# Attention beside an octonion feed-forward: 123 entries of the maxima ahead of attention, not 52, a new order in attention, and a fourth set of queries, keys and values

## The reference

```python
xn = _layernorm(x, axis=-1)
# attention
qkv = einsum('bsd,od->bso', xn, w_qkv) + b_qkv      # 32 heads of 16
scores = einsum('bqhd,bkhd->bhqk', q, k) / sqrt(16) + alibi
attn = softmax(where(causal, scores, -1e9))
s = einsum('bsd,od->bso', attn @ v, w_out) + b_out
# feed-forward, weights ternary, octonion structure
h = silu(gate) * up
g = silu(oct_ternary_linear(h, w_down))
return x + s * g
```

## Time and profile before

| what | value |
|---|---|
| median of 3 runs | 898.8 us (896.7 to 901.62) |
| the profiled execution | 896.58 us, span 894.8 us |
| PE busy | 816.8 us, 91% of the span |
| DVE busy | 630.1 us, 70% |
| ACT busy | 479.1 us, 54% |
| POOL busy | 112.7 us, 13% |
| granted clock of TensorE, mean | 0.979 |
| row maxima on DVE, lines 1083 and 1087 | 512 and 256 instructions, 221.9 and 158.6 us |
| exponentials on ACT, line 806 | 320 instructions, 311.8 us |

### The profile page before, as it was taken

How to read it: one execution, slowest core, us unless ns; L and a number is a source line. 1 busy time by engine, 2 the same in 40 slices (tenths; PEclk the granted TensorE clock), 3 DMA queues, 4 the chain that set the end, 5 groups by cost and what they waited for, 6 DMA issues and landing times.

```text
span 894.8 us, 16075 instructions
## 1 busy us (share of the span) xinstructions
PE 816.8 (91%) x5938; PEld 355.9 (40%) x5938; DVE 630.1 (70%) x1795; ACT 479.1 (54%) x631; POOL 112.7 (13%) x124
## 2 busy tenths in 40 slices
PE   5899989999999999999899899999999999998866
PEld 4445444444444334334343333333333333333322
DVE  5475786643242463463799999999999999992498
ACT  4453265333232221231587778887877778789310
POOL 3123131323031121121000000000000000000042
PEclk8899999999999999999799999999999999999989
DMA  7735322243102000000022111222222111264658
GB/s 218 210 107 177 129 72 82 100 123 94 48 1 71 24 1 24 24 0 30 19 63 75 56 55 55 70 75 75 66 71 75 50 58 56 72 193 125 226 192 314
DMA packets 68199, 80.01 MB, mean 89 GB/s; under 512 B 26630, under 2 KB 38918, under 8 KB 67608
## 3 DMA queue, kind: packets, MB, share of 16 engines
q1 hardware_dynamic: 67992, 78.71, 27.8%
q0 software_dynamic: 128, 0.27, 0.2%
HBM read 46.95 MB, written 31.73 MB: 88 GB/s over the span
## 4 chain that ended last, share of the span: by engine, by line
PE 64%; DVE 16%; issue 8%; DMA 7%; SPq 4%; ACT 2%; POOL 0%; ACTq 0%; DVEq 0%
PE psum L1389 13%; PE psum L1349 9%; PE psum L1412 9%; PE psum L1413 8%; DVE mshown L1083 5%; PE psum L1423 4%; PE psum L1424 4%; DVE mx L1087 4%; PE psum L1365 3%; DMA o_scr<-osum 2%; PE psum L1249 2%; PE psum L1251 2%; PE psum L1250 2%; DMA r_scr<-den 2%; PE psum L1261 2%
## 5 line engine op out<-in xcount | busy, mean ns | idle before, releaser
L806 ACT ACTIVATE probs<-psum,exp_scale 128x1024 f32<-128x1024 f32 (+1 forms) x320 | 311.8, 1028 | 78.4 <-PE psum L1374 48.5
L1083 DVE CUSTOM_DVE_ANT_0 mshown<-psum,ahead 128x384 bf16<-128x384 f32 (+3 forms) x512 | 221.9, 487 | 15.2 <-PE psum L1349 13.9
L1349 PE MATMUL psum<-QKs 51*128 51x512 f16 (+3 forms) x768 | 194.1, 333 | 16.0 <-DVE mx L1083 6.2
L1389 PE MATMUL psum<-probs,Vs 128*32 128x512 f32 (+3 forms) x1536 | 162.3, 510 | 19.8 <-ACT osum L812 17.6
L1087 DVE TENSOR_REDUCE mx<-psum 128x1 f32<-128x512 f32 x256 | 158.6, 683 | 3.2 <-PE psum L1349 2.2
L1365 PE MATMUL psum<-QKs 53*128 53x512 f16 (+3 forms) x768 | 139.5, 331 | 3.3 <-ACT probs L806 3.1
L1412 PE MATMUL psum<-X,room 128*128 128x512 f16 (+1 forms) x352 | 133.9, 380 | 0.0
L1413 PE MATMUL psum<-X,room 128*128 128x512 f16 (+1 forms) x352 | 133.4, 379 | 0.0
L1349 PEld LDWEIGHTS psum<-QKs 51*128 51x128 f16 x768 | 53.2, 94 | 166.4 <-DVE mx L1083 87.8
L831 ACT ACTIVATE room<-psum,gate_half 128x512 f32<-128x512 f32 (+1 forms) x44 | 30.2, 687 | 110.0 <-PE psum L1413 109.9
L1117 DVE SCALAR_TENSOR_TENSOR room<-room,psum 128x512 f32<-128x512 f32 (+1 forms) x44 | 30.2, 687 | 71.3 <-ACT room L831 71.3
(11 more groups left out here) (148 smaller groups left out, 934.4 us busy)
## 6 DMA issues: line engine op xcount, KB each, us to landing
o_scr<-osum SPq DMA_DIRECT2D x32, 256.0 KB, 2.9
QKs<-q_scr SPq DMA_DIRECT2D x96, 64.0 KB
QKs<-k_scr SPq DMA_DIRECT2D x96, 64.0 KB
q_scr<-qk_stage SPq DMA_DIRECT2D x16, 256.0 KB, 2.2
k_scr<-qk_stage SPq DMA_DIRECT2D x16, 256.0 KB, 2.2
v_scr<-v_stage SPq DMA_DIRECT2D x16, 256.0 KB, 2.0
Vs<-v_scr SPq DMA_DIRECT2D x16, 256.0 KB
g_scr<-room SPq DMA_DIRECT2D x16, 256.0 KB, 2.0
```

What stands on the lines that cost most here:

```text
L806: nc.scalar.activation(probs[n % PSLOTS][:, 2 * pair:2 * pair + 2, 0:COLS[n]], s_bank[pair][:, :, 0:COLS[n]], ACT.Exp, scale=exp_scale[:, ...
L1083: last = nc.vector.tensor_tensor_reduce(out=mshown[at % 2][:, cols], in0=m_bank[bank][:, cols], in1=ahead[:, CH - keys:], scale=1.0, scala ...
L1349: last = nc.tensor.matmul(tile[:, hh, :], Qs[s][rows, pair + hh, qb * P:(qb + 1) * P], Ks[s][rows, pair + hh, k0:k0 + keys], start=(hh == ...
L1389: last = nc.tensor.matmul(pv_bank[32 * h:32 * h + 32, CH - cols:CH], Vs[s][:, kb, h::QH], probs[n % PSLOTS][:, h, at:at + cols], start=(kb ...
```

## The change

`SLOTS` is 4. The fourth slot of queries and keys is a view of `X16[0]`; its constants and `load(3)` are issued in the last chunk of the gated stage, once the third chunk's gate and up tiles are done. Group t (from 1 to 12) issues `load(t + 3)`.

`early` now runs up to number 39 of group 2's entries, without entry 5 of group 0. It is given out in runs of three after every second tile, and the last run stands after the last tile. Group t has 37 entries "maximum" in place of 42: group 0 begins at entry 39 of group 2, group 1 at entry 34 of group 3, and each starts five earlier than the one before it, down to entry 11 of group 15 in group 14, which has 32 entries as before. `GROUP` has 67 letters in place of 72, and P, S and M stand in a new order. The work itself, every piece, read, exponential and product, is unchanged.

```diff
--- before.py
+++ after.py
@@ -28,7 +28,7 @@
 HALF = P // 2
 PAIRS = QH // 2
 M_SCALE = 2.0 ** 15
-SLOTS = 3
+SLOTS = 4
 INV_SCALE = 4.0
 
 X_SCALE = 2.0 ** 8
@@ -126,7 +126,6 @@
 FTILES = 2 * HT + TT
 FSIG = HT + TT
 FRING = 5
-F_FIRST = 2 * FTILES
 
 
 def position(u, i):
@@ -139,14 +138,23 @@
     return u * NITEM - 1 + i, (i - 1) % MRING
 
 
-GROUP = "MPMMPSMMSMPMMSSMMMSSMMPMSMMSPMMSMPMM" \
-        "SMSMMPMSMMMMSSMPMMSPMMSSMMPMMSMSMMSM"
+GROUP = "MPMSMMPMSMSMPMMSSMMPMSMMSPMMSMPMM" \
+        "SSMMPMSMMSMPSMMSMPMSMMSMPMSMSMMSMS"
+AHEAD = [LEAD + (QUADS - 2 - t) * (NITEM - GROUP.count("M")) for t in range(QUADS - 1)]
+
+
+def line(t):
+
+    start = (t + 1) * NITEM + AHEAD[t] if t < QUADS - 1 else QUADS * NITEM
+    return start
 
 
 def group_order(t):
 
     scores = [(n, pair) for n in range(NST) for pair in range(2)]
-    items = [(t + 1, i) for i in range(LEAD, NITEM)] + [(t + 2, i) for i in range(LEAD)]
+    items = [divmod(i, NITEM) for i in range(line(t), line(t + 1))] if t < QUADS - 1 else []
+    if t == QUADS - 2:
+        items.append((QUADS, ROWS_AT))
     products = [(t - 1, n) for n in range(NST - LAG, NST)] + [(t, n) for n in range(NST - LAG)]
     out = []
     for kind in GROUP:
@@ -154,21 +162,21 @@
             out.append(("scores", t, *scores.pop(0)))
         elif kind == "P":
             out.append(("products", *products.pop(0)))
-        else:
+        elif items:
             out.append(("maximum", *items.pop(0)))
-    return [w for w in out if w[1] >= 0 and (w[0] != "maximum" or w[1] < QUADS or w[1:] == (QUADS, ROWS_AT))]
+    return [w for w in out if w[1] >= 0]
 
 
 def work_order():
 
-    early = [(0, i) for i in range(NITEM) if i != ROWS_AT] + [(1, i) for i in range(LEAD)]
+    early = [divmod(i, NITEM) for i in range(line(0)) if i != ROWS_AT]
     tiles = [(j, p) for j in range(NCH) for p in range(FTILES)]
     order, given = [], 0
     for n, tile in enumerate(tiles):
         order.append(("ffn", *tile))
-        due = max(n + 1 - F_FIRST, 0) * len(early) // (len(tiles) - F_FIRST)
-        order += [("maximum", *x) for x in early[given:due]]
-        given = max(given, due)
+        if tile[1] % 2 and len(tiles) - n <= 2 * -(-len(early) // MRING):
+            order += [("maximum", *x) for x in early[given:given + MRING]]
+            given += MRING
     for t in range(QUADS):
         for w in group_order(t):
             order.append(w)
@@ -221,7 +229,8 @@
 
         OW = alloc(top, "OW", [P, 2, KT, D], f16)
         X16 = [alloc(top, f"X16{i}", [P, 2, KT, CH], f16) for i in range(2)]
-        QKs = [alloc(top, f"QKs{i}", [P, 2, PAIRS, S], f16) for i in range(SLOTS)]
+        QKs = [alloc(top, f"QKs{i}", [P, 2, PAIRS, S], f16) for i in range(SLOTS - 1)]
+        QKs.append(X16[0][:].rearrange("p a k t -> p (a k t)").rearrange("p (a h t) -> p a h t", a=2, h=PAIRS))
         Qs, Ks = ([x[:, i] for x in QKs] for i in range(2))
         Vs = [alloc(top, f"Vs{i}", [P, KB, 2 * QH * HD], f32) for i in range(SLOTS)]
         mx = [alloc(top, f"mx{i}", [P, 2, PAIRS, KB], f32) for i in range(2)]
@@ -530,18 +539,21 @@
             for i in range(2):
                 sp.wait_ge(qk_stored[i], 16 + NCH * KT * 16)
                 sp.wait_ge(v_stored[i], 16 + NCH * TT // 2 * 16)
-            for i in range(SLOTS):
+            def constants(i):
                 for u in range(2):
                     sp.dma_start(Qs[i][u * HALF + ROWS_QK:u * HALF + ROWS_MAX], c_scr).then_inc(q_ones, 16)
-            for i in range(SLOTS):
+
+            for i in range(SLOTS - 1):
+                constants(i)
+            for i in range(SLOTS - 1):
                 load(i)
 
             def beside(w):
 
                 if w[0] == "scores" and w[3] == 1:
                     t, n = w[1], w[2]
-                    if n == 0 and SLOTS - 2 <= t <= QUADS - 3:
-                        load(t + 2)
+                    if n == 0 and 1 <= t <= QUADS - SLOTS:
+                        load(t + SLOTS - 1)
                     if n == 3 and t > 0:
                         store(t - 1, 1)
                     if n == 6:
@@ -555,6 +567,10 @@
                         store_gated(w[1], w[2] - 2 * HT - 1)
                     if w[2] == 0 and w[1] > 0:
                         store_gated(w[1] - 1, TT - 1)
+                    if w[2] == 1 and w[1] == NCH - 1:
+                        sp.wait_ge(f_filled, (NCH - 2) * FTILES + 2 * HT)
+                        constants(SLOTS - 1)
+                        load(SLOTS - 1)
 
             def denominators(c):
 
@@ -1330,9 +1346,11 @@
                 s = t % SLOTS
                 if i == 0:
                     if t == 0:
-                        pe.wait_ge(q_ones, SLOTS * 2 * 16)
+                        pe.wait_ge(q_ones, (SLOTS - 1) * 2 * 16)
                         pe.wait_ge(evac_done, NCH * TILES)
                     pe.wait_ge(stacked[s], stack_uses(t))
+                if i == 0 and t == SLOTS - 1:
+                    pe.wait_ge(q_ones, SLOTS * 2 * 16)
                 pe.wait_ge(max_read, at + 1)
                 if i == ROWS_AT:
```

## The result

The median after is 927.3 us (four runs, 925.7 to 930.1); the kernel before took 898.7 beside it. The ratio is 1.032, interval 1.028 to 1.036: slower by 3.2%. Forecast were 900 us and a range of 885 to 909; the time lies outside it. The profiled execution took 927.5, its span is 925.7, 30.9 more than before.

The account below looks back on a forecast made before the run. DVE was taken to bound a group at 95%, PE the gated stage. Terms +3.7 + 0.6 - 0.7 - 10.4 + 4.7 + 3.0 + 1.4 = +2.3 us gave 898.9 or 901, stated as 900; range 885 to 909.

Parts of the forecast that it names:

- The gated stage (+3.7): Gated stage: 40 runs of three pieces between tiles cost 23.6 us, against 19.9 for 51 single entries: +3.7.
- The seam and group 0: From gated stage into attention: one more read at the seam, +0.6 us; group 0 gains about an ordinary group's, -0.7.
- the +0.6: Seam: five pieces instead of four ahead of the first scores, one more read of 0.62 us.
- the period of 24.5: Groups 1 to 13: DVE's 21.2 us plus idle 2.3, 0.7 and 0.35 make 24.5 a group, -10.4 us.
- the walk: Attention group: entries priced one by one for DVE's idle time; beyond P(3) and P(0), 0.3 to 0.4 us more.
- rival C: Attention groups: DVE's relief buys nothing, the chain scores, exponential, copy, product sets the period; 25.3 gives 911 us; chance 0.24.
- The clock (+3.0): Group 1: PE's stand of 4.1 us at the load halves the granted clock, as after the seam: +3.0 us.
- +1.4: The end, groups 14 and 15: new order without relief, late P(3) idles ACT; +0.2 and +1.2 us.
- The load (+4.7): Groups 1 and 2: PE waits for the fourth-next set, a load taken as 8.8 us: +4.1 and +0.6.
- rival B: Attention groups: DVE stays the only bound, copy waits hide under its backlog; at 23.0 a group 882 us; chance 0.26.

Follow-up runs that it names:

- e4: Kernel before, its 52 early entries given out in runs of three after every second tile, nothing else: 889.5 us, ratio 0.990.
- e9: Kernel after, DVE reading only 128 columns of each piece, part of the computation left out: 912.7 us, ratio 1.014.
- e1: Kernel after, ACT's two copies of the sums one exponential sooner: 896.4 us, ratio 0.998.
- e6: Kernel after, only the copy ahead of P(3) one exponential sooner: 902.4 us, ratio 1.004.
- e15: e7 with the new order of P and S and 42 entries M: 905.2 us, ratio 1.007.
- e13: e7 with LEAD 16 for 11, so another piece stands at each place of the order: 918.3 us, ratio 1.022.
- e5: e1 with a fifth set in the other X16, loaded ahead of attention, so no piece waits for a set: 883.8 us, ratio 0.984.
- e14: e7 with LEAD 21 for 11, so another piece stands at each place of the order: 897.7 us, ratio 1.000.
- e7: Kernel before with runs of three and both copies of the sums one exponential sooner: 874.1 us, ratio 0.973.

## Why the prediction was wrong

**The gated stage (+3.7) was right:** +4.0. The reading of runs, two switches shared by three pieces and a third piece that costs its columns, gave 23.6 for 40 runs and 10.0 for the 17 of e4; measured were 23.7 and 9.9. The seam and group 0 came within 0.8 us, in part by luck: the fifth piece that the +0.6 stands for isn't there (four stand before the first scores, and from the last full matmul to these it is 2.5 us, 2.6 before), and group 0 has 3.4 us more at half the clock.

**The step that failed is the period of 24.5.** Its parts were there as written: DVE's 21.2, P(3) 3.2 us behind S(4, 0), the waits ahead of P(3) and P(0). Without a fall of the clock the period is 25.3 (25.1 to 25.6). DVE idles about 4.0 in it, not 3.35: its gaps behind P(3) and P(0) are 2.4 together, less than the 3.0 of the forecast, but the rest of the walk, "0.3 to 0.4 more" for all other entries, came to about 1.5. I had walked the order as if DVE stayed the bound and lost time only at two marked places. e9 shows that it did not: with DVE's work halved the group still takes 24.15, so PE and ACT, waiting for each other in this order, hold it just under my figure with little of DVE. Why the full reads then add 1.2 is argued, not shown: PE and ACT on one side and DVE on the other meet in three banks.

By the table of corners, the forecast had 2.9 us for the relief of DVE (24.1 to 21.2) and 2.15 for the gaps of the new order (3.35 for 1.2). Going from the old order to the new one at 42 entries, and then to 37, the runs show 2.5 for either, and nothing is left. By the other way round both are 0.7: the two don't add up, and a sum of one price for each could not show it. The length is that of rival C (25.3 a group), to which I gave 0.24, and so is the part on the waits for the copy. But C's words, that the relief buys nothing, fit the old order (0.7, or 0.2 with the copies sooner) and not the new one. The argument against C, that PE loses five pieces, looked at PE's busy time; the waits go through PE's queue and ACT's.

**The clock (+3.0) was counted once.** Above, it fell in six of the groups 3 to 13. Those took 26.2 on average, the other five 25.3: 0.9 us each, and 0.5 over the mean of the eleven (25.8). Groups 14 and 15 took 9.1 more than before, where +1.4 was forecast; they hold 13.7 us of half clock. An estimate from this: 54.6 us more of attention were at half the clock, 16 times 3.4, at 0.9 each 14 us, with what follows the loads included. I had argued from waits of 1.11 us at full clock that short waits don't matter, and the prediction set the rule that it cites from the Trainium skill aside on that ground. The six falls start 13 to 14 us into their groups, behind the wait for the copy, and with that wait shortened (e1, e6) they are gone. But the length of one wait doesn't decide. Group 5 of the kernel after has the longest wait of the steady groups and kept full speed, e15 waits 1.1 to 1.3 in every group and kept it too, and e13 has none above 0.46 us, with PE busy 24.3 of 26.4, and the clock fell in seven groups of eleven. PE in group 5, its window, and the stands of e13's group 7 with the window of that group:

```profile
593.12 1.09 PE L1407 MATMUL psum<-probs,Vs 128*32 128x512 f32 x8 [2.41 <-ACT osum L828]
580.20:605.80 25.60, 22.12 (x237) 9.12 (x236) 21.09 (x77) 20.44 (x22) 0.00 (x0) 1.00 0.23 65
```

```profile
634.06 0.28 PE L1349 MATMUL psum<-QKs 51*128 51x128 f16 x2 [0.46 <-DVE mx L1083]
634.67 0.28 PE L1349 MATMUL psum<-QKs 51*128 51x256 f16 x1 [0.33 <-DVE mx L1083]
...
635.79 0.39 PE L1349 MATMUL psum<-QKs 51*128 51x256 f16 x2 [0.29 <-DVE mx L1083]
620.70:648.50 27.80, 25.72 (x243) 9.20 (x241) 24.11 (x85) 20.47 (x22) 0.00 (x0) 0.94 0.21 60
```

The Trainium skill (TensorE: Matmul & The Clock Gate, "A second HAM failure mode: psum-queue depth-cycling") says that frequent short idles of PE between groups of matmuls can make its clock go back and forth. These traces agree in kind (group 6: five stands above 0.1 us, 3.2 us idle in all, granted clock 0.94; e13 as above), and I had not weighed it. What makes the clock fall in one group and not in the next stays open, and so does what the falls cost by themselves: no run changed them alone.

**The load (+4.7) was under-sized.** The stands were 5.10 and 2.43, together 7.5: a load takes 9.9 to 10.4, not 8.8. With what follows it (half clock in groups 1 and 2) the price in e5 is 12.6, 10.3 of it in these two groups, measured with the copies sooner; load and clock together had 7.7.

**One figure of rival B doesn't follow from its sum:** 882 without the 3.0 for the clock is 879; 874 is reached only without the 4.7 for the load too.

**What no step named** is the match of pieces and places. With 42 entries each group sees the same piece at the same letter, with 37 they move by five places. e13 and e14 show about 2 us a group (2.15 and 1.75) for the place alone. How much of the 1.2 us above is due to it was not separated.

**Not the change's:** 3.6 us ahead of the gated stage. That stage starts between 179 and 187 us in the runs, with falls of the clock in other places. The -3.7 behind attention is of the same kind, as far as seen.

By cause, as measured: late copies 31, loads 12.6 (with the copies sooner), 70 entries more in the gated stage 13.8 against 9.7 for the runs. The parts overlap in the groups and are not a sum.

## What to carry to other kernels

Before an engine at 95% is relieved, time the loop with much of that engine's work gone: here that run says 23.65 for the old order and 24.15 for the new one, against 25.3, and shows how little there is to gain before an order is kept. In an order by hand, look for the entry that two engines wait on in turn (here a copy queued behind an exponential it doesn't need) and move that first; here it was one digit in two lines, worth 15 us in the kernel with the old order (e4 to e7) and 31 in the new one. And where a fixed order meets work of uneven size through few buffers, the offset between them is a choice of its own: 24.25, 26.0 and 26.4 us for the same work. Try a few on the chip.

## What the runs showed of the hardware

- PE's clock fell to half for 3.4 us in six of eleven groups of attention in which PE is busy 88 to 90% of the time, each 13 to 14 us into its group; the starts at 646.3, 697.5, 748.7 and 799.9 are 51.2 apart. The longest wait of PE in these groups was 1.6 to 2.0 us. It stayed at full speed in a group with a wait of 2.41, and in all steady groups of e15 with up to 1.27 and of e1 with up to 1.40; it fell in seven of eleven groups of e13, where no wait is above 0.46, and in eight of e9, where the longest are 2.1 to 2.4. The length of one wait does not tell.
- Moving between full-height matmuls and pieces on 51 rows costs PE about 0.2 us for in and out together (0.62 for the run at 407.14, less two times 0.216 for its columns); a run of three pays it once, and 17 runs in place of 51 single entries took 9.7 us less (e4). The Trainium skill's rule on weight loads (TensorE: Matmul & The Clock Gate, "The mechanism"), weighed in the prediction, would have put an estimated 4 us more into the gated stage; 0.3 more than forecast were measured.
- A load of a set, 15 DMAs, takes 9.9 to 10.4 us, of which 6.9 go by up to its last issue, most of them about 0.46 apart; the piece that needs it starts 3.0 after that.
